# Waiting for a state product in place of a tanh: the trigger of the row scatters in a recurrent scan

## What is computed

```python
h_new = jnp.tanh(h * leak + gate * z_t)          # first scan, 128 steps, gate from h and z_t
attn  = softmax((q k + relative keys) / sqrt(8))   # 16 heads, relative keys and values
x = x + attention(first scan)
next_h = jnp.tanh(xp_t + prev_h @ Wh)            # second scan, 128 steps: xp = x @ Wx + b
router -> softmax -> top 2 of 8 experts          # per token: 32 * 128 = 4096 tokens
out = sum over the 2 choices of weight * (gelu(h w1 + b1) w2 + b2)
x = x + out
```

## Time and profile before

| | |
|---|---|
| median of three runs | 727.92 us |
| the profiled execution's own time | 724.73 us |
| its span, first to last instruction | 721.8 us |
| second scan, first to last tanh | 428.22 to 549.64 us, 128 steps |
| expert stage | the 172 us behind it |
| TensorE, VectorE, ScalarE, GpSimd busy | 83%, 60%, 54%, 56% of the span |

### The profile page before, as it was taken

How to read it: one execution, slowest core, us unless ns; L and a number is a source line. 1 busy time by engine, 2 the same in 40 slices (tenths; PEclk the granted TensorE clock), 3 DMA queues, 4 the chain that set the end, 5 groups by cost and what they waited for, 6 DMA issues and landing times. The chain is left out here.

```text
span 721.8 us, 27264 instructions
## 1 busy us (share of the span) xinstructions
PE 600.0 (83%) x10479; PEld 454.4 (63%) x10479; DVE 433.5 (60%) x2041; ACT 392.9 (54%) x1112; POOL 400.9 (56%) x433
## 2 busy tenths in 40 slices
PE   3888888888879989999997857777777788999993
PEld 1565555555667766776675734334445777999993
DVE  1666666666557677677765334555545553456775
ACT  4666666666414545555553523222225656899893
POOL 4445554445338878798777421545443656565552
PEclk9999999999979999999999988555556989999997
DMA  7356655555686766677666024333111222225452
GB/s 254 118 207 228 226 186 210 206 205 196 236 246 186 221 177 184 163 217 199 178 182 208 3 88 152 102 97 102 36 54 32 62 79 68 75 75 175 133 160 98
DMA packets 111943, 108.69 MB, mean 151 GB/s; under 512 B 7136, under 2 KB 85472, under 8 KB 111440
## 3 DMA queue, kind: packets, MB, share of 16 engines
q1 hardware_dynamic: 107120, 97.66, 43.0%
q0 software_dynamic: 4320, 8.89, 3.7%
q10 hardware_dynamic: 384, 0.52, 0.2%
HBM read 59.43 MB, written 45.52 MB: 145 GB/s over the span
## 5 line engine op out<-in xcount | busy, mean ns | idle before, releaser
L515 POOL TENSOR_TENSOR sc<-sc,mx 128x1024 f32<-128x1024 f32 x64 | 121.2, 1899 | 53.2 <-DVE mx L673 53.2
L406 POOL TENSOR_SCALAR QD<-q_all,mask 128x128 f32<-128x128 f32 x126 | 88.8, 717 | 98.0 <-DVE pre L361 94.9
L673 DVE CUSTOM_DVE_ANT_0 sc<-banks,s2t 128x128 f32<-128x128 f32 x512 | 112.0, 286 | 49.6 <-PE banks L566 48.2
L1203 POOL DMA_INDIRECT expert_outputs<-yr,xr x71 | 78.5, 1106 | 67.1 <-DVE yr L1471 33.8
L731 ACT ACTIVATE PT<-banks 128x512 f32<-128x512 f32 x128 | 69.8, 596 | 64.2 <-PE banks L579 64.2
L1195 POOL DMA_INDIRECT expert_inputs<-rows,slotu x64 | 63.5, 992 | 68.5 <-ACT h L1125 49.6
L1143 ACT ACTIVATE hid<-banks,w1b 128x128 f32<-128x128 f32 x284 | 81.0, 368 | 24.6 <-PE banks L1086 17.7
L352 DVE COPY s2stage<-banks 128x512 f32<-128x512 f32 (+1 forms) x90 | 76.6, 852 | 16.5 <-PE banks L253 16.5
L1125 ACT ACTIVATE h<-banks,bias 128x32 f32<-128x32 f32 x128 | 36.8, 288 | 86.4 <-PE banks L420 80.2
L1086 PE MATMUL banks<-xt,w1b 128*128 128x128 f32 x568 | 78.0, 282 | 6.8 <-DVE xt L1421 6.8
L1107 PE MATMUL banks<-w2b,hid 128*128 128x128 f32 x568 | 78.4, 283 | 5.3 <-ACT hid L1143 4.9
(11 more groups left out here) (144 smaller groups left out, 1062.7 us busy)
## 6 DMA issues: line engine op xcount, KB each, us to landing
s_scratch<-s2stage SPq DMA_DIRECT2D x32, 1024.0 KB, 4.8
s2t<-s_scratch SPq DMA_DIRECT2D x64, 512.0 KB, 4.9
xr<-expert_inputs SPq DMA_DIRECT2D x71, 64.5 KB
xz<-in_xz SPq DMA_DIRECT2D x8, 512.0 KB, 5.7
yb<-expert_outputs SPq DMA_DIRECT2D x16, 256.0 KB
w2all<-in_w2b SPq DMA_DIRECT2D x8, 320.0 KB
w1a<-in_w1b SPq DMA_DIRECT2D x8, 258.0 KB
k_all<-in_xT SPq DMA_DIRECT2D x1, 2048.0 KB, 11.2
```

The source lines that it names most:

```text
L406: op = pool.tensor_scalar(QD[G % 3][:, :, h, :], q_all[:, :, quad(G)].rearrange("p b t -> p t b"), mask[:, h:h + 1], None, ALU.mult)
L515: pool.tensor_tensor(sc[U % RING][:], sc[U % RING][:], mx[U % RING][:].unsqueeze(2).broadcast_to([P, HH, T]), ALU.subtract)\
L673: op = dve.tensor_tensor_reduce(out=sc[r][:, h, :], in0=ps[2 * (U % 2) + h // 4][:, h % 4 * T:(h % 4 + 1) * T], in1=s2t[r][:, h, :], scale ...
L1203: pool.indirect_dma_start(yg_dram, bass.IndirectOffsetOnAxis(xr[k][:, D:].bitcast(U32), 0), yr[k][:], None).then_inc(s_ys[k], 16)
```

## The change

It touches two lines. The step number of each scatter grows by one, and GpSimd waits for the semaphore of the state products in place of that of the tanh.

```diff
         def scatter_step(c, k):
 
-            return (c + 1) * TC + 10 + 2 * k
+            return (c + 1) * TC + 11 + 2 * k
```

```diff
                     for k in range(2 * JT):
                         if scatter_step(c, k) < T:
-                            pool.wait_ge(s_h2, scatter_step(c, k) + 1)
+                            pool.wait_ge(s_r, scatter_step(c, k) + 1)
                             scatter(c, k)
```

## The result

The changed kernel takes 728.97 us (median of 20 runs, 724.0 to 733.12), the kernel before 724.60 us in 20 runs beside it (719.49 to 728.98). The ratio is 1.0076 with a 95% interval of 1.0059 to 1.0094. The forecast was 717 us, from a base of 727.92 us that three runs had given. The profiled execution has a span of 727.8 us against 721.8.

A forecast was written before the change was run, and what follows sets the result against it. The product-tanh chain, held by GpSimd scatters, bounds the second scan. Middle chunks save 1.97 us times 5, 9.8, and chunk 7 saves 1.2: 11.0 off 727.92 gives 716.9, told as 717 us, range 703 to 731.

The forecast's parts named there:

- What bounds the kernel: Second scan: the chain product, tanh, product bounds it, and a product's signal is held while GpSimd works on a scatter.
- The first tanh of a pair: First tanh behind a single scatter: delayed 0 to 0.11 us; the pair then takes 1.61 us against 1.92, saving 0.31.
- S: Start of a single scatter after the change, about 0.25 us after a tanh starts; the next tanh is due 0.49 later.
- the slower rival: Single scatters: the first tanh is caught too, a pair takes 2.39 us in place of 1.92, time 748 us; chance 0.17.
- The head: Start of a chunk's scatters, scatters 0 and 1: 1.84 us over in place of 2.77, bounds 0.3 and 2.77.
- 11.84: A chunk of the second scan without scatter delays: sixteen steps of 0.74 us make 11.84 us.
- the single pairs: Two steps around each single scatter: 0.13 us of delay left per pair, six pairs a middle chunk, 0.8 us.
- the no-gain rival: Second scan: each scatter takes 0.44 us from the chain wherever it starts; time stays at 728 us; chance 0.18.
- likeliest case: Whole kernel: shorter pairs and chunk starts give 717 us, own range 709 to 724; chance 0.48.
- The clock: Rival for the second scan: TensorE's clock comes back, at most 6 us more gained, 703 to 709 us; chance 0.17.
- Costed at nothing: Same instructions and far-off waits cost 0; if the scan's end met the first output scatter, at most 0.96 us.

The follow-up runs named there:

- scan_alone: Kernel before with a rows and slots buffer per chunk and chunk 0 to 6 scatters issued behind the scan: 757.53 us in all, scan 87.6 us against 121.4.
- product_10: Kernel before with only the wait changed, from the tanh to the state product, at the old step numbers: 713.71 us, ratio 0.9840.
- product_11_even: Changed kernel with the router's logits and positions matmuls moved by one step: 679.25, 679.89, 680.05 and 679.94 us, ratios 1.0040, 1.0031, 1.0034 and 1.0063 to the kernel before.
- product_10_lead: Kernel before with the wait on the state product and a one-instruction GpSimd fill between the two waits: 678.36, 678.07 and 679.17 us, ratios 1.0002, 0.9987 and 1.0010.

## Why the prediction was wrong

**What bounds the kernel: right where holds are seen, and only there.** Scatters hold state products: on chip 12 the scan is 34 us shorter without them (scan_alone). On three of five chips no such holds are seen, and on the one of them where the change itself was run (3) it is worth nothing (0.9997). A single trace could not tell that. The rule that I set aside, of the Trainium skill, page "SBUF — State Buffer", section "Who interferes with whom", that PE and ACT never wait on anyone, agrees with the traces of chips 1, 3 and 9 and not with those of 11 and 12, if it is read as widely as the prediction read it. The page speaks of ports of the SBUF, and no row here says that a port is behind the holds. By it the time would have been 728, which is nearer to the result than my forecast, though for another reason: gains and losses of a few us each that nearly cancel.

**The step that failed: the first tanh of a pair.** The prediction took the signal due at S + 0.49 as free or heard at S + 0.60, and saved 0.31 a pair. In steps 2 to 10 it was caught in 27 places of 30, at S + 1.29 to + 1.45, 0.8 to 0.95 late: the pair is 2.3 us. This is the mechanism of the slower rival, which I gave 0.17 and priced at 2.39 a pair from the earlier trace rows. The choice between a row at + 0.42 (free) and one at + 0.52 (caught) was made for the wrong one. What I had no idea of is that steps differ: product_10, with the same phase and the steps changed over, has the pair of 1.75 us and takes 713.7 us, 12 us less than the kernel before. So the phase argument was right for odd steps, and for the sixth pair of the changed kernel, around j = 0: that pair takes 1.65 us in chunk 4 (485.66 to 487.31), where 1.61 was forecast. It was wrong for the even steps 2 to 10, and the change as made puts its scatters ahead of these. What makes them different stays open. Extra matmuls ahead of them is a guess: the product at j = 4 is caught with no logits in the step before, that at j = 10 of chunk 7 is free with them, and product_11_even met no chip with holds.

**The head: too high.** Forecast 1.84, measured 0.76. Scatter 0 did start 0.75 behind the tanh of step 11 (481.83, 482.58). The tanh of step 13 was not on time at + 0.73 but 0.61 late; by this scatter 1, which waits for a product, started only 1.58 behind scatter 0, so in chunks 2 to 6 the two did not bunch. A wait on the chain that is held spaces the scatters by itself. In chunk 7, where step 12 has no filler behind its product, the tanh of step 13 was on time, and the forecast for every head came to pass:

```profile
550.81 0.99 POOL L1195 DMA_INDIRECT expert_inputs<-rows,slotu  x1 [1.22 <-PE banks L420]
...
551.54 0.29 ACT L1125 ACTIVATE h<-banks,bias 128x32 f32<-128x32 f32 x1 [0.45 <-PE banks L420]
...
552.11 0.96 POOL L1195 DMA_INDIRECT expert_inputs<-rows,slotu  x1 [0.30 <-issue]
...
553.62 0.29 ACT L1125 ACTIVATE h<-banks,bias 128x32 f32<-128x32 f32 x1 [1.79 <-PE banks L420]
```

Step 13 on time at + 0.73, the second scatter 1.30 behind the first, step 14 due at + 0.17 and heard at + 1.51, 1.34 late. The prediction's sum left the head of chunk 7 out.

**The sum.** For chunk 3: 11.84 + 4.35 + 0.76 = 16.95 of the measured 17.2; the rest is two tanh, of j = 1 and 15, each 0.11 late. (The 11.84 fits chunk 0 before by chance: its steps take 0.67 to 0.75 us, and one takes 1.21, the tanh of step 6 at 432.88, before any scatter of the scan. So late tanh ahead of the first scatter were not absent, as the prediction says; scan_alone keeps this one and one other.) The head gave back 2.0 and the single pairs took 2.15, which with this rest makes the chunk 0.3 longer than before, 16.9. In chunk 4 the kernel before had a cheaper head and the changed one a dearer, and the loss is 2.35. In chunk 7 four caught tanh cost 3.45 where four late ones cost 1.9 before, and its head, 1.5 in place of 1.0, adds most of the rest: 16.4 against 14.2, where 1.2 less was forecast. In all the scan takes 5.9 us more, where 11.0 less were forecast. By these terms it is the single pairs that were mis-sized: 0.13 of delay for each was forecast, about 0.87 was measured.

**What was luck.** The measured 728.97 us lies inside the outer range of 703 to 731 only because the no-gain rival had drawn it that wide, from a base 3.3 us above the median of the 20 runs. The likeliest case's own 709 to 724 misses it, and the time moved the other way.

**The clock.** That it might come back was a rival; after the change it stayed at 0.50 in chunks 2 to 5. product_10 had 0.62 with shorter holes, scan_alone 0.98 and the changed kernel on chip 3 1.00 with none. The direction of that rival was right in the runs with few or no holes.

**Costed at nothing:** the end of the scan against the first output scatter, and VectorE's slots. The slots came in time (scatter 0 starts 0.75 behind its tanh). The two kinds of scatter did not meet: GpSimd stood idle 7.57 us between them. The expert stage is 1.2 us longer all the same; one execution of each kernel does not tell whether the change or their spread makes it.

## What to carry to other kernels

A profile of one chip may show a cost that other chips do not have. Before an order is tuned around a wait with no visible resource, time the same program on several chips: here the difference is 47 us, while the edits are worth 4 to 12.

When the trace shows a catch at some phases and steps, tabulate every occurrence by phase and by step before moving anything (the trace of before already had a product due at + 0.18 held to + 1.28 at j = 14), and test the two halves of a change apart: of this one, the wait alone gained 1.6% on chip 12 and the step number turned it into a loss.

## What the runs showed of the hardware

- Beside a GpSimd indirect DMA of 128 rows (0.96 us), a TensorE product's signal that was late was heard 1.29 to 1.60 us behind the start of a single scatter (traces of before, the change, and chips 11 and 12); on chips 1, 3 and 9 this pattern is absent, even with scatters 1.26 us apart. No row shows the resource.
- The wait for the product at the old step numbers (product_10) gives 0.984 on chip 12. On the others it was not run by itself; with the one-instruction lead it gives 1.0002, 0.9987 and 1.0010 (chips 9, 3 and 1).
- An indirect DMA behind two waits starts 0.77 us behind the end of the releasing tanh, or 0.75 behind the signal of the releasing product; with a one-instruction fill between the waits it starts 0.27 behind the tanh, and the kernel takes 0.994 of the time on chip 12.
- The granted clock of the middle chunks is 0.50 with the longest holes between products, 0.62 with shorter ones (product_10) and 0.98 with none (scan_alone). A low clock is not needed for a hold nor enough for one: a product was caught at 1.00 (448 to 451 of the kernel before), and others were free at 0.54 (463.7 to 470.4 of product_10_lead).
